# The last sum inside layer 0's first LayerNorm moves from VectorE to GpSimd, as one operation per chunk

## The reference

```
q, k, v = x Wq' + bq, x Wk' + bk, x Wv' + bv            # 4 heads of 64
scores  = clip(q k' / 8, -10, 10), -10 where adj == 0
attn    = softmax over each 256 keys by itself          # 8 segments of keys
ctx     = sum over the segments of attn v
out     = ctx Wo' + bo + x
out     = (out - mean) * rsqrt(var + 1e-5) * gamma + beta     # first LayerNorm
x1      = LayerNorm(x + out), without gamma and beta          # second LayerNorm
```

## Time and profile before

| | us |
|---|---|
| median of 3 runs | 3712.26 |
| lowest, highest | 3709.11, 3714.05 |
| the profiled execution | 3715.06 |
| its span | 3713.2 |

### The profile page before, as it was taken

How to read it: one execution, slowest core, us unless ns; L and a number is a source line. 1 busy time by engine, 2 the same in 40 slices (tenths; PEclk the granted TensorE clock), 3 DMA queues, 4 the chain that set the end, 5 groups by cost and what they waited for, 6 DMA issues and landing times. The chain is left out here.

```text
span 3713.2 us, 135473 instructions
## 1 busy us (share of the span) xinstructions
PE 3538.6 (95%) x57302; PEld 2495.4 (67%) x57302; DVE 2930.0 (79%) x3447; ACT 2545.3 (69%) x3746; POOL 2244.2 (60%) x1152
## 2 busy tenths in 40 slices
PE   5999999999999999999999999996599999999998
PEld 2656766665665676567566666653478888888886
DVE  6687787678678767767867876885699999999986
ACT  2666666666666666656666666664488889898887
POOL 1797788688778878878977887896021212212220
PEclk9999999999999999999999999997799999999999
DMA  6010010001001000100100100001122122122211
GB/s 231 3 37 15 20 37 14 15 21 43 15 14 37 20 15 21 36 14 15 43 14 20 37 20 14 14 20 47 46 58 69 47 81 69 58 69 69 58 35 57
DMA packets 128571, 145.48 MB, mean 39 GB/s; under 512 B 29777, under 2 KB 113617, under 8 KB 125905
## 3 DMA queue, kind: packets, MB, share of 16 engines
q1 hardware_dynamic: 126704, 136.14, 11.4%
q10 hardware_dynamic: 1248, 0.40, 0.1%
HBM read 102.70 MB, written 33.75 MB: 37 GB/s over the span
## 5 line engine op out<-in xcount | busy, mean ns | idle before, releaser
L403 ACT ACTIVATE probs<-probs 128x1024 f32<-128x1024 f32 x1024 | 1083.6, 1058 | 768.0 <-DVE probs L865 747.0
L281 POOL TENSOR_TENSOR psums<-probs 128x1024 f32<-128x1024 f32 x512 | 1253.1, 2448 | 462.6 <-ACT probs L403 461.5
L515 PE MATMUL ctx_ps<-probs,v_rows 64*32 64x512 f32 x16256 | 1475.8, 590 | 7.1 <-DVE seg_ctx L802 5.3
L865 DVE SCALAR_TENSOR_TENSOR probs<-sc_ps,edges 128x1024 f32<-128x1024 f32 x1024 | 1226.1, 1218 | 311.7 <-PE sc_ps L502 301.6
L502 PE MATMUL sc_ps<-q_cols,k_cols 64*32 64x512 f32 x16384 | 1200.6, 590 | 22.1 <-DVE probs L865 21.7
L1414 PE MATMUL out_ps<-wh,e 128*128 128x257 f32 x4096 | 927.6, 382 | 50.8 <-DVE e L1541 48.6
L1414 PEld LDWEIGHTS out_ps<-wh,e 128*128 128x128 f32 x4096 | 773.9, 191 | 170.3 <-issue 40.7
L515 PEld LDWEIGHTS ctx_ps<-probs,v_rows 64*32 64x32 f32 x16256 | 665.0, 106 | 279.5 <-issue 182.6
L502 PEld LDWEIGHTS sc_ps<-q_cols,k_cols 64*32 64x32 f32 x16384 | 549.2, 107 | 298.0 <-issue 176.0
L509 PE MATMUL den_ps<-psums,ones 64*32 64x512 f32 x4064 | 600.1, 591 | 13.9 <-DVE seg_ctx L802 7.9
L305 POOL TENSOR_TENSOR ctx_t<-ctx_t,seg_ctx 128x1024 f32<-128x1024 f32 x224 | 545.0, 2433 | 52.3 <-DVE seg_ctx L802 52.1
(11 more groups left out here) (96 smaller groups left out, 3181.4 us busy)
## 6 DMA issues: line engine op xcount, KB each, us to landing
x_cols<-in_xT SPq DMA_DIRECT2D x8, 2048.0 KB, 7.9
probs<-in_adjT SPq DMA_DIRECT2D x16, 1024.0 KB, 8.6
x_rows<-in_x SPq DMA_DIRECT2D x32, 512.0 KB, 3.9
x<-res SPq DMA_DIRECT2D x32, 512.0 KB, 2.9
x_in<-x SPq DMA_DIRECT2D x32, 512.0 KB, 4.4
x_res<-x SPq DMA_DIRECT2D x32, 512.0 KB, 4.8
out<-h SPq DMA_DIRECT2D x32, 512.0 KB, 3.2
high<-rows SPq DMA_DIRECT2D x16, 512.0 KB, 4.1
```

The costliest lines, as they stand in the source:

```text
L281: pool.tensor_tensor(psums[:, q % 2, pair, :], probs[:, (SJ * q) % RING, pair, :], probs[:, (SJ * q + 1) % RING, pair, :], ALU.add).then_i ...
L403: act.activation(probs[:, n % RING, pair, :], probs[:, n % RING, pair, :], ACT.Exp, scale=DH ** -0.5).then_inc(s_exp, 1)
L515: return pe.matmul(ctx_ps[quad(h), z, :], v_rows[head_rows(r), n % JB, at:at + QUAD], probs[head_rows(r), n % RING, h, :], start=start, st ...
L865: dve.scalar_tensor_tensor(out=probs[:, n % RING, pair, :], in0=sc_ps[:, p, :, :], scalar=-LIM, in1=clip_hi[:, j, c * CW:(c + 1) * CW][:, ...
```

## The change

`add_x` leaves VectorE's block and becomes an operation of GpSimd over the whole chunk (128x1024), after the second partial sum of block 1. It waits for both gamma products; x + beta is GpSimd's own and comes earlier in its order. s_z now counts one per chunk. VectorE takes the four statistics and the aggregate together in block 3, GpSimd's second inverse deviation goes from block 3 to block 4, behind x + beta, and ScalarE's second normalisations from blocks 4 and 5 to 5 and 6. The tail changes likewise.

```
+            def add_x(b, c):
+                pool.wait_ge(s_gam, count(b, 2 * NC, 2 * c + 2))
+                pool.sem_inc(s_pool_waited, 1)
+                pool.tensor_tensor(res[:, c % 2, :, :], res[:, c % 2, :, :], x_rows[:, c % 2, :, :], ALU.add)\
+                    .then_inc(s_z, 1)
+                pool.wait_ge(s_z, count(b, NC, c + 1))
+                pool.sem_inc(s_xfree, 1)
...
-                    if k == 3 and prev == 2:
+                    if prev == 2 and k == 1:
+                        add_x(*back(b, c - 2, NC))
+                    if k == 4 and prev == 2:
                         inverse_deviation(*back(b, c - 2, NC), 1)
             def tail(b):
                 add_bo(b, NC - 1)
                 sum_segment(b, SEGS - 1, 0)
                 sum_segment(b, SEGS - 1, 1)
+                add_x(b, NC - 2)
...
                 inverse_deviation(b, NC - 1, 0)
+                add_x(b, NC - 1)
                 inverse_deviation(b, NC - 1, 1)
...  (ScalarE)
-                    if prev == 2 and k in (4, 5):
-                        norm(*back(b, c - 2, NC), 2 * (k - 4), 1)
+                    if prev == 2 and k in (5, 6):
+                        norm(*back(b, c - 2, NC), 2 * (k - 5), 1)
...  (VectorE)
-            def add_x(b, c, half):
-                two = slice(2 * half, 2 * half + 2)
-                dve.wait_ge(s_gam, count(b, 2 * NC, 2 * c + 1 + half))
-                dve.wait_ge(s_xbeta, count(b, NC, c + 1))
-                dve.tensor_tensor(res[:, c % 2, two, :], res[:, c % 2, two, :],
-                                  x_rows[:, c % 2, two, :], ALU.add).then_inc(s_z, 1)
-                if half == 1:
-                    dve.wait_ge(s_z, count(b, 2 * NC, 2 * c + 2))
-                    dve.sem_inc(s_xfree, 1)
...
-                    if prev == 2 and k == 1:
-                        add_x(*back(b, c - 2, NC), 1)
-                    if prev == 2 and k == 2:
+                    if prev == 2 and k == 3:
+                        stats(*back(b, c - 2, NC), 0)
+                        stats(*back(b, c - 2, NC), 1)
                         stats(*back(b, c - 2, NC), 2)
                         stats(*back(b, c - 2, NC), 3)
...
-                    if prev == 2 and k == 0:
-                        add_x(*back(b, c - 2, NC), 0)
-                    if prev == 2 and k == 1:
-                        stats(*back(b, c - 2, NC), 0)
-                        stats(*back(b, c - 2, NC), 1)
-                    if prev == 2 and k == 2:
-                        variance(*back(b, c - 2, NC), 1)
...
+                    if prev == 2 and k == 3:
+                        variance(*back(b, c - 2, NC), 1)
                     clip(b, n + 1, 0)
...
                 times_gamma(b, c - 1, 1)
-                add_x(b, c - 1, 0)
                 normalise(b, SEGS - LAG)
-                add_x(b, c - 1, 1)
+                normalise(b, SEGS - 1)
                 for t in range(T):
                     stats(b, c - 1, t)
-                normalise(b, SEGS - 1)
...
                     times_gamma(b, c, half)
-                for half in range(2):
-                    add_x(b, c, half)
```

More of the change, by code:

```diff
@@ L382, in norm @@
                     if which == 1:
-                        act.wait_ge(s_z, count(b, 2 * NC, 2 * c + 2))
+                        act.wait_ge(s_z, count(b, NC, c + 1))
                 act.activation(res[:, c % 2, t, :], res[:, c % 2, t, :], ACT.Identity,
@@ L423, in chunk @@
                         norm(*back(b, c - 1, NC), 2 * (k - 6) + 1, 0)
-                    if prev == 2 and k in (4, 5):
-                        norm(*back(b, c - 2, NC), 2 * (k - 4) + 1, 1)
+                    if prev == 2 and k in (5, 6):
+                        norm(*back(b, c - 2, NC), 2 * (k - 5) + 1, 1)
                     if second:
@@ L814, in stats @@
             def stats(b, c, t):
-                dve.wait_ge(s_z, count(b, 2 * NC, 2 * c + 1 + t // 2))
+                dve.wait_ge(s_z, count(b, NC, c + 1))
                 dve.bn_stats(bn[:, 1, t, :], res[:, c % 2, t, :]).then_inc(s_bn[1], 1)
```

## The result

| | median us (runs) | lowest to highest |
|---|---|---|
| before | 3712.12 (17) | 3703.96 to 3717.57 |
| after | 3718.90 (17) | 3713.37 to 3726.23 |

The ratio is 1.0019 with a 95% interval of 1.0011 to 1.0027: slower by 4 to 10 us. The profiled execution of after took 3720.66 us, its span is 3718.9 (before 3715.06 and 3713.2).

A forecast was written before the change was run, and what follows sets the result against it. TensorE was taken as the bound, plus VectorE's delays at the chunk start in kinds 2 and 3. Costs of 30.8 us less gains of 28.2 gave net +2.6, so 3715 us, no change that can be told; range 3698 to 3733.

The forecast's parts named there:

- kind 0: Chunks of kind 0: no excess that could be placed, and GpSimd's lateness absorbed, so 0.
- the race: Block 0, kinds 2 and 3: gamma's product would get in before GpSimd's add, giving back 4.3 us.
- rival (1): Block 7: gamma's product is hit by GpSimd's adds where the sum was; slower, 3735 us, chance 0.27.
- VectorE's relief: Blocks 0 and 1: VectorE's 64 sums go, and with them their collisions with GpSimd's adds; 23.9 us gained.
- The late deviation: Second inverse deviation, 1.71 us, in GpSimd's gapless run from block 4: TensorE stalls in block 6 or 7, costing 28.3 us.
- The rival that GpSimd's lag is free (2): GpSimd's run is not late, as TensorE's reserve is larger or vanished collisions save GpSimd more; 3698 us, chance 0.23.
- The step in VectorE's block 3: Aggregates before the third clip push it back some 0.35 us, so GpSimd's gapless run starts 0.35 later.
- The sum on GpSimd: Block 1: one more add, net 1.95 us per chunk; 1.2 us of stall in kind 2, 1.0 in the last chunk.
- The tail: End of layer 0: two sums of together 1.29 us become one of 2.4 plus a semaphore hop, +1.3 us.

The follow-up runs named there:

- the repeat: The changed kernel run once more, unchanged, for a second trace: 3716.43 us.
- the one tried: Changed kernel with gamma's first product in block 7 moved from before the third clip to behind the normalise: 3754.48 us, ratio 1.0119.
- the five kernels below 3690 us: Before without the sum: 3684.84; change with deviation in block 3: 3688.21, or x + beta there: 3689.48; these two with gamma's second product behind the second clip: 3678.70, 3677.79.

## Why the prediction came out

The forecast was an exchange of two effects of nearly 30 us, and it was one. The median moved by +6.8 us where some +2.7 was forecast. The ratio of 1.0019 lies just within the 0.2% that were called no change, but its interval (1.0011 to 1.0027) reaches over that line and excludes 1: a small loss is now told that the prediction left open.

That the total came so near owes something to luck. The mechanisms of the two large terms are shown by the experiments. But the 5 us of kind 0, foreseen as 0, stand against the 4.3 of the race that was counted on and did not come, and the stalls alone are less than the 28.3 us foreseen; gamma's long products, which only rival (1) had, make up the rest.

- **VectorE's relief, 23.9 us predicted.** Left out alone, the sums give 26 us, in the loop 9.0 in kind 2 (10.3 predicted) and 9.8 in kind 3 (9.6). The 2.2 us taken for each of four kind 2 chunks were misread by a little: these were 2.9 us over 69.15 in the mean, which less the 0.5 gives 2.4, and with the sums left out they give 1.6 to 2.2. The mechanism is the one named: an operation of VectorE behind a GpSimd add, clips behind it, and the exponentials, the reciprocal and the normalise behind them. Kind 0 was mis-sized: I found no excess there, and it gave 5.1 us in the change and 3.6 with the sums left out. Kind 3 gave less than 1.6 each, 1.5 in the loop, and none outside.
- **The late deviation, 28.3 us predicted.** Alone it costs 30 us, and 31 us come back when it is undone in the change. The stall is 1.6 to 1.7 us in kind 1, as 1.8 was read from the reserve of 0.4 us at 1455.91. Blocks 6 and 7 of the 16 short chunks are 1.4 to 1.8 us longer where no product is held, 26 us together (an estimate from the change's two traces); the four long products add 1.9 us each and 4.3 in the last chunk. The rival that GpSimd's lag is free (2) is refuted by the 34 waits for psums.
- **The step in VectorE's block 3, 0.35 us.** It was 0.13: the clip starts that much later, counted from the statistics before it. What hides the other 0.2 isn't shown in kind 1; in the last chunk of the kernel before, the same clip waits 0.18 us for TensorE's scores.
- **The sum on GpSimd.** Some 3 us with all that moved beside it. The kind 2 chunks of the loop take 9.52 to 9.56 us in block 3 where they mostly took 9.44, against 0.15 expected; but with the sum left out three of them take 9.68 there, so that this is the sum's price isn't shown. In the last chunk block 3 is 11.65 us in both traces of the change, 9.58 before and 9.58 with no sum: 2.1 us where 1.0 was estimated.
- **The race.** It turned hardly anywhere. In the loop the product of block 0 in kinds 2 and 3 still takes 2.7 to 2.9 us (but for the kind 2 chunks that start the second and third round, where it was shorter before too), against the prediction's sign of less than 1 us. GpSimd's first sum there (1145.28) waits for an exponential, by which its lag is gone: the add behind it starts 0.07 us ahead of the product, as before. Elsewhere the product got in first (0.8 us) in one chunk of the first trace and in two of the repeat; each follows a chunk whose product in block 7 was held, and two of the three are some 0.7 us shorter, one 0.4. So the turn is worth what was estimated, but nearly all of the 4.3 us never came. That more could be had is shown by moving the product: 9.5 us less by the medians, 7 by the ratios, which allow for the kernel before as it ran beside each.
- **The slower rival (1)** came true in small. Four of gamma's products in block 7, in four different chunks, took 3.2 us (three) and 5.5 us, and the last chunk is 75.1 us instead of the 71 expected. The 5.54:

```profile
2540.42 5.54 DVE L840 TENSOR_TENSOR res<-res,gamma_r 128x512 f32<-128x512 f32 x1
2545.89 1.21 DVE L867 SCALAR_TENSOR_TENSOR probs<-sc_ps,edges 128x1024 f32<-128x1024 f32 x1
```

```profile
2538.39 2.38 POOL L313 TENSOR_TENSOR ctx_t<-ctx_t,seg_ctx 128x1024 f32<-128x1024 f32 x1
2540.73 2.37 POOL L281 TENSOR_TENSOR psums<-probs 128x1024 f32<-128x1024 f32 x1
2543.07 2.34 POOL L288 TENSOR_TENSOR res<-x_rows,bo_r 128x1024 f32<-128x1024 f32 x1
```

It starts while GpSimd is at 2538.39, does not get in at 2540.73 nor at 2543.07, and ends 0.55 us after that add. The prediction had taken it that VectorE gets in when the add ends that it met. The distance between the two traces of the change in the last chunk (75.1 and 70.8) is this one event: its block 7 takes 12.98 and 8.72 us.

- **The tail.** The statistics start 2.55 us after the last gamma product (1.36 before): +1.2 us, for +1.3 predicted. The whole stretch to layer 1 is 43.0 and 42.7 us in the two traces of the change, and 43.6 and 40.7 in those of before; with the sum left out it is 40.5. So the tail seems to cost about 2 us, and the first trace of before was long there for a reason that isn't shown.

```profile
2577.58 0.69 DVE L840 TENSOR_TENSOR res<-res,gamma_r 128x512 f32<-128x512 f32 x1 [0.29 <-ACT res L396]
2580.82 1.41 DVE L828 BATCH_NORM_STATS2 bn<-res 128x6 f32<-128x256 f32 x4 [2.55 <-POOL res L300]
```

Three things remain open. What makes the kind 2 chunk that starts the second and the third round 0.6 to 4 us longer than its kind, in every trace, wasn't tried. Layer 1's 1.8 us between the traces lie within what its length varies among the runs here (1127 to 1131 us). And it wasn't tried whether a place exists for gamma's first product in block 7 that is safe from being held through two or three adds; the one tried was worse.

## What to carry to other kernels

An engine at 60% of the span can be without a gap for four stages in a row: read its timeline from the last wait to the next, and the distance between its result and the taker's start. That distance is all it can take, and here moving 1.7 us from a place with 2.5 us of idle time to one without cost 30 us, where the moved sum itself, with what moved beside it, cost about 3. When two effects of opposite sign come in one change, split it: the half that was worth having was 23 us, and 31 with gamma's product moved, hidden behind the other.

## What the runs showed of the hardware

- A 128x512 float32 product or sum of VectorE with both inputs in SBUF takes 0.68 us, and 2.7 to 2.9 when it arrives just after a GpSimd add of 2.38 us began; the GpSimd add after it takes 2.83. The Trainium skill (SBUF — State Buffer, "Who interferes with whom") calls it an exclusive lock, and for one add these numbers agree.
- Not expected: the end of the GpSimd operation doesn't always let VectorE in. If GpSimd's next add starts at once, VectorE may wait through it (3.2 us) or through two more (5.5 and 6.3 us). The traces of the kernel before have one such operation each, those of the change four and three, the one with the deviation alone moved nine, and the five kernels below 3690 us none.
- The order of arrival within 0.1 us decides 2.2 us (2.87 us at 0.07 us behind GpSimd, 0.68 when the add started at 2096.46, 0.01 us behind the product), and it can be the same in every round of a loop: in the kernel before 10.8 us for block 0 of one kind 2 chunk in each of three rounds, in both traces, and 9.6 outside the loop, from the same instructions.
